# Attention's squares: eight wide steps of a pass by VectorE, one instruction a step, in a ring of six steps

## The reference, cut to what matters

```python
scores = jnp.einsum('bhqd,bhkd->bhqk', q, k) * hs ** (-0.5)   # 4 batches, 16 heads of width 16
p = jax.nn.softplus(scores)
p = p * p
causal = jnp.tril(jnp.ones((t, t), dtype=p.dtype))
p = p * causal
attn = p / (jnp.sum(p, axis=-1, keepdims=True) + 1e-09)
out = jnp.einsum('bhqk,bhkd->bhqd', attn, v)
```

## Time and profile before

| what | value |
|---|---|
| median of three runs | 1626.35 us |
| profiled execution | 1625.58 us |
| its span | 1623.7 us |
| TensorE, whole span | 1524.7 us busy (94%) |
| VectorE | 1247.4 us (77%) |
| ScalarE | 853.9 us (53%) |
| GpSimd | 694.7 us (43%) |
| VectorE's squares in attention, L1429 | 144 instructions, 320.2 us |
| GpSimd's squares in attention, L1492 | 112 instructions, 314.8 us |
| ScalarE's softplus, L1403 | 288 instructions, 268.1 us |

### The profile page before, as it was taken

How to read it: one execution, slowest core, us unless ns; L and a number is a source line. 1 busy time by engine, 2 the same in 40 slices (tenths; PEclk the granted TensorE clock), 3 DMA queues, 4 the chain that set the end, 5 groups by cost and what they waited for, 6 DMA issues and landing times. The chain is left out here.

```text
span 1623.7 us, 29032 instructions
## 1 busy us (share of the span) xinstructions
PE 1524.7 (94%) x11188; PEld 1122.8 (69%) x11188; DVE 1247.4 (77%) x2386; ACT 853.9 (53%) x1356; POOL 694.7 (43%) x478
## 2 busy tenths in 40 slices
PE   8999888899999897999999999988999999799998
PEld 7888776444444443988877787766777777678787
DVE  5554896999999999565568888767877777677886
ACT  3333487777777785433333222258888887421210
POOL 0002112999999998400234222112655555211111
PEclk9999999999999999999999999999999999999999
DMA  4000166667756770000010000012333332100000
GB/s 160 21 1 14 35 193 168 100 88 97 101 78 93 97 103 4 10 5 1 13 40 20 1 1 1 1 55 80 105 106 105 105 106 105 40 14 26 14 26 27
DMA packets 57017, 95.80 MB, mean 59 GB/s; under 512 B 7760, under 2 KB 29488, under 8 KB 56880
## 3 DMA queue, kind: packets, MB, share of 16 engines
q1 hardware_dynamic: 55920, 93.35, 26.1%
q10 hardware_dynamic: 960, 0.59, 0.1%
HBM read 76.88 MB, written 17.04 MB: 58 GB/s over the span
## 5 line engine op out<-in xcount | busy, mean ns | idle before, releaser
L1429 DVE TENSOR_TENSOR att_weights<-att_weights 128x1024 f32<-128x1024 f32 x144 | 320.2, 2246 | 11.3 <-ACT att_weights L1403 11.3
L1492 POOL TENSOR_TENSOR att_weights<-att_weights 128x1024 f32<-128x1024 f32 x112 | 314.8, 2843 | 4.8 <-ACT att_weights L1403 3.4
L1403 ACT ACTIVATE att_weights<-ps 128x1024 f32<-128x1024 f32 (+1 forms) x288 | 268.1, 976 | 81.6 <-PE ps L1345 50.9
L927 DVE SCALAR_TENSOR_TENSOR X<-ps,moe_gsel,X 128x256 f32<-128x256 f32 x512 | 246.0, 483 | 72.7 <-PE ps L48 50.6
L48 PE MATMUL ps<-w_experts_hi,moe_xh 128*128 128x512 f32 x512 | 204.0, 399 | 0.0
L48 PE MATMUL ps<-w_experts_hi,moe_xl 128*128 128x512 f32 x512 | 203.2, 397 | 0.0
L48 PE MATMUL ps<-w_experts_lo,moe_xh 128*128 128x512 f32 x512 | 201.5, 393 | 0.0
L1363 PE MATMUL ps<-att_weights,att_v_ones 64*32 64x64 f32 (+5 forms) x2048 | 159.8, 401 | 29.6 <-DVE v L1450 15.6
L424 ACT ACTIVATE ffn_gates<-ps,ffn_gate_bias 128x512 f32<-128x512 f32 x72 | 49.6, 689 | 148.2 <-PE ps L48 128.7
L1363 PEld LDWEIGHTS ps<-att_weights,att_v_ones 128*32 128x32 f32 (+1 forms) x2048 | 53.4, 108 | 97.6 <-issue 49.3
L996 POOL TENSOR_TENSOR X<-X,moe_bias_sb 128x512 f32<-128x512 f32 x32 | 41.4, 1294 | 184.9 <-DVE X L927 162.3
(11 more groups left out here) (282 smaller groups left out, 3679.8 us busy)
## 6 DMA issues: line engine op xcount, KB each, us to landing
ssm_lb<-decays SPq DMA_DIRECT2D x32, 512.0 KB, 4.7
ssm_rise<-decays SPq DMA_DIRECT2D x28, 512.0 KB, 3.8
qk_parts<-qkv_part SPq DMA_DIRECT2D x32, 384.0 KB, 2.8
q_stack<-qk_parts SPq DMA_DIRECT2D x64, 128.0 KB, 4.9
k_stack<-qk_parts SPq DMA_DIRECT2D x64, 128.0 KB, 8.3
att_q_stack<-qk_parts SPq DMA_DIRECT2D x64, 128.0 KB, 4.9
att_k_stack<-qk_parts SPq DMA_DIRECT2D x64, 128.0 KB, 8.7
out<-X SPq DMA_DIRECT2D x7, 512.0 KB, 2.9
```

The source lines that it names most:

```text
L927: dve.scalar_tensor_tensor(out=x, in0=ring[:, e // 2, (e % 2) * C:(e % 2 + 1) * C], scalar=gsel[:, s, j, e:e + 1], in1=x, op0=ALU.mult, op ...
L1403: act.activation(Wt[:, u % WU, 0:n], scores(u)[:, 0:n], ACT.Softplus).then_inc(plus_done, 1)
L1429: dve.tensor_tensor(wt, wt, wt, ALU.mult).then_inc(sq_dve, 1)
L1492: pool.tensor_tensor(wt, wt, wt, ALU.mult).then_inc(sq_pool, 1)
```

## The change

The ring of weights is kept by steps in place of units: `Wt` has six slots (`WS`) of two units each, the same 12 units of memory; a half-width step takes a whole slot. The square is done once for a step: `engine_of` is a table over steps, ScalarE keeps steps 2 and 9, and VectorE takes the other eight, each as one instruction of 128x2048 behind the softplus of the step's last unit. GpSimd squares nothing. A value step waits for one semaphore count in place of one for each unit, and softplus waits for the value step six steps back.

```diff
-    SU, WU = 3, 12
+    SU, WS = 3, 6
...
-    BY_DVE, BY_POOL, BY_ACT = range(3)
-    engine_of = [BY_ACT if BANKS[u % PU] == 1 else BY_POOL if u % PU in (1, 3, 6, 8, 10, 13, 15) else BY_DVE for u in range(NU)]
-    squares = [[sum(engine_of[x] == e for x in range(u)) for u in range(NU + 1)] for e in range(3)]
+    step_begin = [0] + [end + 1 for end in step_end[:-1]]
+    BY_DVE, BY_ACT = range(2)
+    ACT_STEPS = (2, 9)
+    engine_of = [BY_ACT if m % PS in ACT_STEPS else BY_DVE for m in range(NS)]
+    squares = [[sum(engine_of[x] == e for x in range(m)) for m in range(NS + 1)] for e in range(2)]
...
-        Wt = sb("weights", [P, WU, 2, BANK], F32)
+        Wt = sb("weights", [P, WS, 2, 2, BANK], F32)
...
+        def weights_of(i, m):
+            wide = BANKS[step_end[m] % PU]
+            return Wt[:, (i * NS + m) % WS, 0:step_end[m] + 1 - step_begin[m], 0:wide]
...
-                for u in range(base + products[0][2], base + last + 1):
-                    pe.wait_ge(squared[engine_of[u]], i * squares[engine_of[u]][NU] + squares[engine_of[u]][u + 1])
+                made = squares[engine_of[m]]
+                pe.wait_ge(squared[engine_of[m]], i * made[NS] + made[m + 1])
...
-                before = step_of[u - WU] + NS if u >= WU else step_of[u - WU + NU]
-                act.wait_ge(pv_done, i * NS + before + 1)
-                n = BANKS[u % PU]
-                act.activation(Wt[:, u % WU, 0:n], scores(u)[:, 0:n], ACT.Softplus).then_inc(plus_done, 1)
+                m, n = step_of[u], BANKS[u % PU]
+                if i * NS + m >= WS:
+                    act.wait_ge(pv_done, NS + i * NS + m - WS + 1)
+                act.activation(weights_of(i, m)[:, u - step_begin[m]], scores(u)[:, 0:n], ACT.Softplus).then_inc(plus_done, 1)
...
-            def square(i, u):
+            def square(i, m):
...
-                dve.wait_ge(plus_done, SU + i * NU + u + 1)
-                wt = Wt[:, u % WU, 0:BANKS[u % PU]]
+                dve.wait_ge(plus_done, SU + i * NU + step_end[m] + 1)
+                wt = weights_of(i, m)
                 dve.tensor_tensor(wt, wt, wt, ALU.mult).then_inc(sq_dve, 1)
...
-                    if engine_of[u] == BY_DVE:
-                        square(i, u)
+                    if u == step_end[step_of[u]] and engine_of[step_of[u]] == BY_DVE:
+                        square(i, step_of[u])
...
-                    if engine_of[u] == BY_POOL:
-                        pool.wait_ge(plus_done, SU + i * NU + u + 1)
-                        wt = Wt[:, u % WU, 0:BANKS[u % PU]]
-                        pool.tensor_tensor(wt, wt, wt, ALU.mult).then_inc(sq_pool, 1)
```

More of the change, by code:

```diff
@@ L1283, in attention_phase @@
     TURN_LAG, COPY_LAG, DEN_LAG, OUT_LAG = 4, 7, 9, 10
-    SU, WU = 3, 12
-    assert NU % SU == 0 and NU % WU == 0
-    BY_DVE, BY_POOL, BY_ACT = range(3)
-    engine_of = [BY_ACT if BANKS[u % PU] == 1 else BY_POOL if u % PU in (1, 3, 6, 8, 10, 13, 15) else BY_DVE for u in range(NU)]
-    squares = [[sum(engine_of[x] == e for x in range(u)) for u in range(NU + 1)] for e in range(3)]
+    SU, WS = 3, 6
+    assert NU % SU == 0
+    step_begin = [0] + [end + 1 for end in step_end[:-1]]
[3 more added lines that the diff above has]
+    squares = [[sum(engine_of[x] == e for x in range(m)) for m in range(NS + 1)] for e in range(2)]
     def outputs_at(x, ends, n, lag, i, first, stage):
@@ L1349, in value_step @@
                 s, (qb, last, products) = m // PS, pass_steps[m % PS]
-                base = s * PU
                 if m % PS == 0:
@@ L1363, in value_step @@
                     ins = pe.matmul(O(qb)[h * 2 * HD:(h + 1) * 2 * HD, q0:q0 + w], values,
-                                    Wt[rows, (base + unit) % WU, t, c:c + w], start=kj == 0 and part == FULL, stop=part == UPPER and kj == (qb + 1) * GT - 1)
+                                    Wt[rows, (i * NS + m) % WS, s * PU + unit - step_begin[m], t, c:c + w], start=kj == 0 and part == FULL, stop=part == UPPER and kj == (qb + 1) * GT - 1)
                 ins.then_inc(pv_done, 1)
@@ L1375, in body @@
                 for m in range(NS):
-                    begin, end = step_end[m - 1] + 1 if m else 0, step_end[m] + 1
+                    begin, end = step_begin[m], step_end[m] + 1
                     for u in range(begin, end):
@@ L1408, in _ @@
             act.sem_inc(plus_done, SU)
-            def square(i, u):
-                act.wait_ge(plus_done, SU + i * NU + u + 1)
-                wt = Wt[:, u % WU, 0:BANKS[u % PU]]
+            def square(i, m):
+                act.wait_ge(plus_done, SU + i * NU + step_end[m] + 1)
+                wt = weights_of(i, m)
                 act.activation(wt, wt, ACT.Square).then_inc(sq_act, 1)
@@ L1417, in _, with square @@
                     softplus(i, u)
[L1418 to L1421, removed]
+                    m = step_of[u] - 1
+                    if u == step_begin[m + 1] and m >= 0 and engine_of[m] == BY_ACT:
+                        square(i, m)
+                if engine_of[NS - 1] == BY_ACT:
+                    square(i, NS - 1)
         @block.vector
         def _(dve):
-            def square(i, u):
-                dve.wait_ge(plus_done, SU + i * NU + u + 1)
-                wt = Wt[:, u % WU, 0:BANKS[u % PU]]
+            def square(i, m):
+                dve.wait_ge(plus_done, SU + i * NU + step_end[m] + 1)
+                wt = weights_of(i, m)
                 dve.tensor_tensor(wt, wt, wt, ALU.mult).then_inc(sq_dve, 1)
```

3 lines of the change are left out of this document (1 added, 2 removed).

## The result

| | before | after |
|---|---|---|
| median of four runs | 1625.74 us (1624.38 to 1626.57) | 1590.08 us (1589.29 to 1591.19) |
| profiled execution | 1625.6 us | 1590.39 us |
| attention, the middle stretch below | 374.94 us | 339.33 us |
| one pass in its steady form | 22.85 us, in the second half of attention 23.01 to 23.18 | 20.69 us |

The ratio is 0.9776 with a 95% interval of 0.9762 to 0.9791: 35.7 us less, where 29.8 were forecast.

A forecast was written before the change was run, and what follows sets the result against it. GpSimd, never resting, was taken to set the 22.85 us pass. Fifteen passes give -28.1 us, the last pass -2.2 and +0.5: -29.8 on 1625.6, 1595.8, stated as 1596; range 1588 to 1611.

The forecast's parts named there:

- three limits: In attention: VectorE's list, TensorE's list and the loop through all three, at 20.3 to 21.0 us; 20.9 taken.
- a little more is won: Rival, chance 0.13: TensorE's work is 20.6 us, copies of v fall into VectorE's rests; pass 20.5, time 1590.
- The rival in which 2246 was the price of a square: VectorE's squares: 2246 ns is cost, not waiting; pass 38.5 us, time about 1870; chance 0.02.
- VectorE's pass: Eight squares at 2.2 us, outputs 2.60, division's wait 0.1, copies of v at most 0.47 + 0.26: 20.3 to 21.0.
- The rival with 22.1 us: VectorE sets the pass, squares of 2048 costing 2.3 to 2.44 us: time 1613, lower end 1605; chance 0.24.
- TensorE's pass: TensorE's work from value step 3 to the next pass's, without its four waits: 20.75 to 20.96 us.
- The loop: From value step 3 through next pass's scores, softplus, squares and division to its value step 3: 20.5 to 21.0 us.
- the slower rival: Copies of v land whole, 2.88 us, on the loop at step 3's square: pass 23.4, time 1633; chance 0.06.
- the clock: Two stretches of TensorE at half clock in attention stay, costing 1.7 us each after the change.
- The passes: 15 attention passes by 20.9 us, 313.5; 316.9 with half clock, against 345.0 before: -28.1 us.
- Costed at nothing: Ring, squares' wait for both units, copies' wait, loads (17.4 to 20.2 us, within 20.9) and first pass: no cost.
- The ends: Last pass: clearing product to value step 3, -2.2 us; from there to the last copy, +0.5 us.

The follow-up runs named there:

- E7: The kernel before the change with GpSimd's squares left out, only its count raised: 1591.99 us, ratio 0.9805.
- E1: The changed kernel with GpSimd's copies of v left out from the third pass on: 1590.76 us, ratio 0.9784.
- E3: The changed kernel with VectorE squaring only the first half of step 8's weights: 1588.64 us, ratio 0.9771.
- E11: E8 with the 16 loads of a pass kept but issued in eight pairs behind scores units: 1584.58 us, ratio 0.9741.
- E9: The changed kernel with the loads of scores' stacks left out from the fifth pass on: 1587.77 us, ratio 0.9767.
- E8: The changed kernel with ScalarE squaring the first unit of step 8 and the bank-clearing product left out: 1590.12 us, ratio 0.9789.
- E2: The changed kernel without the products that mask the rest tiles of the diagonal on TensorE: 1588.63 us, ratio 0.9774.
- E12: The changed kernel, nothing left out, with the 16 loads of a pass issued in eight pairs: 1588.87 us, ratio 0.9773.
- E6: The changed kernel with step 6's square given back to GpSimd as one instruction of 128x2048: 1592.71 us, ratio 0.9809.

## Why the prediction was right, and where it was off

The mechanism and the three limits came out as forecast. The point forecast, 1596, was 6 us too high, and 1590 is the number of the rival "a little more is won". That is chance: its two conditions didn't hold, as TensorE's list takes 20.68 and not 20.6, and the copies of v cost VectorE 0.42 us a pass.

- **The two engines shut each other out: right.** 2246 ns became 1229 when GpSimd was silent (E7), and the wide square came at 2.20 in the queue as taken, with 128 of them 292 us (forecast: some 290). The rival in which 2246 was the price of a square is refuted.
- **VectorE's pass, 20.3 to 21.0: right, 20.69.** Its parts are 17.54 for eight squares by distances of starts (forecast 17.6), 2.73 for the outputs (forecast 2.60 + 0.1), and 0.42 for the copies of v (bound 0.73). The rival with 22.1 us had the right engine for half of the answer and the wrong size; its lower end is 1608 by its own terms, not 1605.
- **TensorE's pass, 20.75 to 20.96: a little too high.** It is 20.68 (E1, E3). I had taken 0.2 us for four waits that are counted from modelled ends; it was nearly 0.3.
- **The loop, 20.5 to 21.0: right at its lower end, and not longer than the other two.** It is the limit of E11, which lightens both engines and no part of the loop: in each of its even passes value step 3 starts 0.05 us after the division has ended, and the pass is 20.50.

```profile
391.18 0.42 DVE L1463 TENSOR_TENSOR v<-ps,att_den 128x256 f32<-128x256 f32 x1
...
391.65 1.06 PE L1370 MATMUL ps<-att_weights,att_v_ones 128*32 128x512 f32 x8
```

  The copies of v, which the slower rival put on the loop with 2.88 us, are recorded with 3.1 in the changed kernel and cost 0.42.
- **The term that failed: the clock.** The sum has 3.4 us for the two stretches at half clock of the earlier trace rows, as if they stayed. In the kernel before each comes right behind a standstill of TensorE, which waits there for a division, longer than the 0.40 us of the earlier trace rows. TensorE's busy time in the 2 us before each is 0.17 and 0.00:

```profile
472.00:474.00 2.00, 0.17 (x4) 0.16 (x8) 2.00 (x3) 1.18 (x2) 2.00 (x2) 1.00 0.51 61
...
564.00:566.00 2.00, 0.00 (x0) 0.00 (x0) 2.00 (x3) 1.20 (x2) 2.00 (x2) 1.00 0.39 47
```

  After the change that wait is gone, and between 281 and 614.6 us the granted clock is 1.00, so the term measured nothing. I treated the clock as a property of the program's place; it stood behind a wait that the change removes. Not every such wait is followed by half clock:

```profile
518.00:520.00 2.00, 0.00 (x0) 0.00 (x0) 2.00 (x3) 1.19 (x2) 2.00 (x2) 1.00 0.16 23
520.00:523.50 3.50, 3.48 (x34) 1.44 (x35) 3.50 (x3) 1.72 (x2) 3.44 (x3) 1.00 0.02 5
```

  Why the division is late wasn't tried. It is so from 451 us on, where TensorE stood still for 1.04 us without a releaser: value step 3 then waits 0.5 to 2.3 us in every pass, and the passes are 24.91 once and 23.01 to 23.18 after that. So the prediction's reading that the 2.25 us over 15 passes are the two stretches was wrong in part: passes without such a stretch were longer too.
- **The passes: 15 x 20.9 forecast, 15 x 20.79 measured**, that is 20.69 and 1.67 us for the two uneven ones, less 0.2 for shorter ones. With the 3.4 us of the clock this is the 5.1 us by which 316.9 missed 311.8.
- **Costed at nothing: the loads.** No engine waits for one to land, as argued. But they cost 1.7 us in the profiled run by the stalls (none in E9), and hid the whole gain of E8.
- **The ends: small.** The last pass's value step 3 is 2.4 us nearer to the clearing product (forecast 2.2); from there to the last copy nothing changed (forecast +0.5).

The tie itself was better seen than its consequence: with equal limits an edit of one of them shows nothing, as E1, E2 and E3 then found.

## What to carry to other kernels

When two engines' records both double wherever they overlap, add up what each takes alone: one engine doing all the work may be faster than two that shut each other out, and what of the other's hold falls beside work that doesn't need the lock costs little. When two engines are full at once, lighten both before judging an edit, and look at the distances of single passes, not at their mean: a gain can be eaten by a few uneven ones. Loads that are early enough may still disturb when they are issued all at once, so try them in smaller groups.

## What the runs showed that was not expected

- TensorE stands still for 0.3 to 2.4 us near the end of a row of 16 loads, with no releaser in the profile; eight pairs in place of one row end it (E11, E12: 13 passes within 0.02 us). Each standstill ends shortly behind a 16 KB packet of the instruction queue.
- The granted clock fell to half (0.51 and 0.53) behind three standstills of 2.1 to 2.4 us, two in the kernel before and one in E8, but not behind another of 2.26 us (at 518 us before). Where it falls, a stall costs more than its own length: the pass at 555 us in E8 took 24.51 us in place of 20.50, with a standstill of 2.4.
- A 128x2048 square on GpSimd, recorded with 4.59 us, costs VectorE's next square 0.95 us and the pass 0.16 (E6).
